# Six score banks of an attention kernel in three groups of two instead of four and two

## The chip, the cores and the metric

The kernel runs on one core of a Trainium2 chip. The metric is the time of one execution on the device in microseconds (us); less is better. The core's engines run side by side and meet through semaphores: TensorE (PE: matmuls, and PEld: the loading of their stationary operand), VectorE (DVE), ScalarE (ACT), GpSimd (POOL) and SyncE (SP), which issues most of the DMAs. An engine works through its own instructions in order.

## What is computed

The input is one sequence of 2048 tokens of width 128. After a layer norm two parts run on it, and both are added to the input: an attention of 16 heads of width 8, and a mixture of 8 experts with the best 2 for each token.

```python
q = proj(Wq) * mod
k = proj(Wk) * mod
v = proj(Wv) * mod
scores = jnp.einsum('bhid,bhjd->bhij', q, k) / math.sqrt(D)
scores = scores * cos_mat
w = jax.nn.softmax(scores, axis=-1)
w = (w + jnp.roll(w, 1, axis=-1)) / math.sqrt(2.0)
out = jnp.einsum('bhij,bhjd->bhid', w, v)
...
h1 = x_rep @ w1[e].T
a, g = jnp.split(h1, 2, axis=-1)
he = jax.nn.silu(a) * g @ w2[e].T
```

## The kernel before

**Scores.** A head's scores are 2048 x 2048, made in 64 tiles of 128 keys x 512 queries; 16 heads give 1024 tiles. One tile is one matmul (line 1381) with 49 rows of contraction, and fills one bank of PSUM. Two neighbours use different row halves of TensorE (`tile_position`) and run side by side, as a pair. Six banks, 0 to 5, hold scores; tile n goes to bank n % 6. Bank 6 is shared by all side work, bank 7 collects the weighted values.

**Exponentials.** ScalarE takes the exponential of a group of tiles with one ACTIVATE (line 706) out of PSUM and writes the result to one of 18 slots a tile in SBUF (`probs`). A round is six tiles, in two groups: a large one of four tiles (banks 0 to 3) and a small one of two (banks 4 and 5). There are 171 rounds; the last has four tiles.

**Weighted values.** TensorE multiplies the exponentials by the head's values (line 1402), four tiles (a quad) at a time in two halves, and adds them up in bank 7. In round r it takes pieces of tiles of rounds before r. At a head's end DVE copies the sums out (line 1046) and normalises them.

**Order.** Each engine's stream is written out round by round. TensorE in round r: `scores` of each group, a maximum job if one is due (line 1417: a score-like matmul of the last two heads, of which DVE takes the maximum, line 1065), then the pieces of weighted values, then the expert's step, then a second job in the rounds 27 to 44. From round 45 on, 39 tiles of tokens go through their experts, three rounds each: step 0 is the result of the tile before (line 1324) and, in 28 tiles, one job; step 1 is the first half of the wide matmuls (line 1311), after which ScalarE does a tanh (line 698); step 2 is the second half. ScalarE's stream: the exponentials of a round, then in step 1 the tanh.

**Waits.** TensorE's `scores(g)` waits until the exponentials up to group g - 2 are done (line 1372): the group that used the same banks in the round before. `weights(g)` on ScalarE waits for the scores of its group (`score_ready`, counted by groups) and until the probability slots are free (`pv_done`). TensorE's weighted values wait for `exp_done`, counted by `groups_for`. SP loads the operands of a head two heads ahead, in a round and behind a count of score groups that come from `groups_for` too (lines 518 to 521).

Of the kernel before, what the change touches and what calls it, by code (L numbers as in the profile page):

```python
# [55 lines left out]
ROWS = 2 * D  # L56
KQ = 1 + 3 * ROWS
HALF = S // 2
LARGE_GROUP, SMALL_GROUP = 4, 2
RING = LARGE_GROUP + SMALL_GROUP  # L60
PROBS = 3 * RING
PER_HEAD = NT * NC
SCORE_TILES = H * PER_HEAD
QUADS = PER_HEAD // NC
HALVES = 2
HW = CW // HALVES
SCORE_GROUPS = 2 * (SCORE_TILES // RING) + -(-(SCORE_TILES % RING) // LARGE_GROUP)
ROUNDS = -(-SCORE_TILES // RING)
SIDE_BANK = 6
V_BANKS = (7, 5)  # L70
# [52 lines left out]
def build(nc, x, Wq, Wk, Wv, Wo, phase, amp, wqkv, w1, w2, ident_in, desc_in, cs_in, sel_in, tri_in, below_in, count_in, heads_in, earlier_in, of_head_in, places_in, out):  # L123
# [3 lines left out]
    whole = nc.dram_tensor("whole_qk", [2, H, ROWS, S], F32, kind="Internal").ap()  # L127
# [7 lines left out]
    with ExitStack() as ctx:  # L135
# [3 lines left out]
        def sem(name):  # L139
            return ctx.enter_context(nc.semaphore(name))  # L140
# [143 lines left out]
        score_ready, exp_done, pv_done, vh_ready = (sem(n) for n in ("score_ready", "exp_done", "pv_done", "vh_ready"))  # L284
# [13 lines left out]
        def after(eng, signal, value):  # L298

            if not (isinstance(value, int) and value <= 0):  # L300
                eng.wait_ge(signal, value)

        def first_of(g):

            return min(RING * (g // 2) + LARGE_GROUP * (g % 2), SCORE_TILES)

        def group_tiles(g):

            return range(first_of(g), first_of(g + 1))

        def bank_of(n):

            return n % RING

# [13 lines left out]

        def groups_for(n):

            whole, rest = divmod(n, RING)
            return 2 * whole + -(-rest // LARGE_GROUP)

        def quads_for(n):

# [27 lines left out]
        def expert_step(r):  # L363

            m, step = divmod(r - EXPERTS_AT, ROUNDS_A_TILE)
            return (m, step) if 0 <= m <= TILES and step < 3 else (None, None)
# [5 lines left out]
        def rounds():  # L372

            done = 0
            for r in range(ROUNDS + 1):
                ready = min(RING * r, SCORE_TILES) // NC * HALVES
                head_ends = (done // (QUADS * HALVES) + 1) * QUADS * HALVES
                even = RING * HALVES * r // NC - 1
                pieces = range(done, max(min(ready if r == ROUNDS else min(ready, even), head_ends), done))
                done = pieces.stop  # L380
                yield r, jobs_of_round(r), pieces
            assert done == H * QUADS * HALVES
# [4 lines left out]

        def groups_of_round(r):

            return range(2 * r, min(2 * r + 2, SCORE_GROUPS))  # L390

        def load_operands(eng, h, q, k, half, loaded):

# [16 lines left out]
        def _(sp):  # L410
# [21 lines left out]
            def store_part(i, part):  # L432
                if part == 0:
                    sp.wait_ge(hi_ready, i + 1)
                else:
                    sp.wait_ge(parts_ready, i + 1)
                g, which = i // 2, i % 2
                sp.dma_start(scratch[which, 8 * g:8 * g + 8, part, :, :].rearrange("h r n -> r h n"),
                             parts[:, i, part, :]).then_inc(scratch_wr, 16)
# [4 lines left out]
            def load_head(p):  # L444
                sp.wait_ge(order_ready, 1 if p < EARLY else 2)
                sp.wait_ge(shift_wr, 16 if p < EARLY else 32)
                if p >= EARLY:
                    sp.wait_ge(scratch_wr, 8 * 16)
                h = sp.value_load(head_order[0:1, p:p + 1], min_val=0, max_val=H - 1)
                for half in range(2):  # L450
                    load_operands(sp, h, qa[p % 2], ka[:, p % 2, :], half, aug_ld[p % 2])
                    load_shift(p, h, half)
# [39 lines left out]
            def store_shifts(g):  # L492
                sp.wait_ge(shift_ready, g + 1)
                sp.dma_start(shift_rows[HALF_HEADS * g:HALF_HEADS * g + HALF_HEADS, :].rearrange("h (t p) -> (h t) p", p=P),
                             shift[:, g, :]).then_inc(shift_wr, 16)
# [19 lines left out]
            for r, _, _ in rounds():  # L515
                m, step = expert_step(r)
                for p in range(2, PLAIN):
                    issued = groups_for(PER_HEAD * (p - 1))
                    if r == -(-issued // 2):
                        sp.wait_ge(score_ready, issued)  # L520
                        load_head(p)
                if r - 1 in PARTS_AT:
                    for part in range(2):
                        store_part(2 + PARTS_AT.index(r - 1), part)
                if r == SECOND_AT + 4:
                    store_shifts(1)
                    sp.wait_ge(scratch_wr, 8 * 16)
                    sp.wait_ge(rows_ready, 2)
                    sp.wait_ge(order_ready, 2)
                    for i in range(EXACT):  # L530
                        h = sp.value_load(head_order[0:1, PLAIN + i:PLAIN + i + 1], min_val=0, max_val=H - 1)
                        for half in range(2):
                            load_operands(sp, h, qe[:, i, :], ka[:, 2 + i, :], half, exact_ld)
                if r == STAGE_AT:
                    for first in range(STAGES - 1):
                        stage_weights(first)
                if r == EXPERTS_AT - 2:
                    load_rows(0)
                    load_rows(1)
                    sp.dma_start(carried[:], slots_x[0:TILES * P, DM:WITH_PLACE].rearrange("(n p) k -> p n k", p=P)).then_inc(carried_ld, 16)  # L540
                if step == 1 and m + STAGES - 1 < TILES:
                    stage_weights(m + STAGES - 1)
                if step == 1 and m % 2 == 1 and m // 2 + 2 < ROW_PAIRS:
                    load_rows(m // 2 + 2)
                if r == EXACT_AT:
                    load_exact_shifts()
# [631 lines left out]
        def _(pe):  # L1178
# [190 lines left out]

            def scores(g):  # L1370

                after(pe, exp_done, g - 1)
                for n in group_tiles(g):
                    p, o, c, b = tile_at(n)
                    if n % PER_HEAD == 0 and p < PLAIN:
                        pe.wait_ge(aug_ld[p % 2], (p // 2 + 1) * 10 * 16)
                    elif n % PER_HEAD == 0:
                        pe.wait_ge(exact_shift_ld, EXACT * 2 * 16)
                    q, k = operands(p)
                    at = 64 * b  # L1380
                    ins = nc.tensor.matmul(ps[:, bank_of(n), :], k[at:at + KQ, P * o:P * o + P], q[at:at + KQ, CW * c:CW * c + CW],  # L1381
                                           start=True, stop=True, tile_position=(at, 0))
                ins.then_inc(score_ready, 1)
# [151 lines left out]
```

## Time and profile before

| | |
|---|---|
| Runs of the kernel | 579.5, 580.15, 581.8 us; median 580.15 |
| Profiled execution | 581.95 us, its span 580.1 us |
| TensorE, ScalarE, VectorE, GpSimd busy | 533.1, 506.9, 222.9, 92.8 us |
| Exponentials (line 706) | 341, busy 474.3 us |
| Granted TensorE clock, mean | 0.982 of full speed |

All durations come from the profiled execution. A busy share is an average; where ScalarE or TensorE sits idle before an instruction, a row's last column has that idle time and what ended it. Two instructions of one engine can overlap in the record, the end of one with the start of the next, so the distance between two starts is less than a duration.

### The profile page before, as it was taken

To read this page: it belongs to the slowest core of one execution; us is meant where nothing else is said; L and a number is where in the kernel's file an instruction comes from. 1 tells how busy PE (TensorE), PEld (TensorE's weight loads), DVE (VectorE), ACT (ScalarE), POOL (GpSimd) and SP (SyncE) were. 2 spreads that over 40 slices of the span, in tenths; PEclk is the share of its full clock that TensorE was granted. 3 is DMA by queue.
4 is the path that set the end of the run, shared out by engine and by line. 5 is a ranking of instruction groups with operands and counts; after the bars stand their busy time and mean duration, and the time that the engine had idled before them with its cause. 6 is when DMAs were issued, how large, how long until landed. Compare 5 with 4: busy or idle time off the path is not lost.

```text
span 580.1 us, 18927 instructions
## 1 busy us (share of the span) xinstructions
PE 533.1 (92%) x7964; PEld 260.2 (45%) x7964; DVE 222.9 (38%) x521; ACT 506.9 (87%) x411; POOL 92.8 (16%) x102
## 2 busy tenths in 40 slices
PE   2969999879999999999999999999999999999876
PEld 1442333323334555454554545555454555554325
DVE  6866356525445242323324232333323132132142
ACT  2649999979899899899999999999999999999971
POOL 5210266530000101011010101110110110101000
PEclk9978999989999999999999999999999999999997
DMA  7962054461014333233324333233324323300402
GB/s 219 193 181 79 20 139 115 110 195 47 2 40 67 88 106 96 88 97 96 97 71 113 98 95 97 86 97 88 106 80 104 98 54 97 92 13 11 139 13 76
DMA packets 60889, 53.75 MB, mean 93 GB/s; under 512 B 33244, under 2 KB 50294, under 8 KB 60546
## 3 DMA queue, kind: packets, MB, share of 16 engines
q1 hardware_dynamic: 58082, 47.48, 30.9%
q0 software_dynamic: 2272, 4.72, 2.3%
q8 instruction: 65, 1.06, 0.8%
q10 hardware_dynamic: 448, 0.30, 0.3%
q14 instruction: 22, 0.18, 0.1%
HBM read 38.68 MB, written 13.78 MB: 90 GB/s over the span
## 4 chain that ended last, share of the span: by engine, by line
PE 44%; issue 25%; ACT 21%; DVE 4%; DMA 2%; SPq 2%; ACTq 0%; DVEq 0%
PE ps L1402 20%; ACT big L706 20%; PE ps L1381 11%; PE ps L1324 4%; PE ps L1417 3%; PE ps L1200 1%; ACT cs L698 1%; PE ps L1351 1%; PE ps L1311 1%; DMA qk_parts<-store 1%; DVE store L789 1%; DMA acc<-in_L_attn_x 1%; DVE m L1065 1%; PE ps L1211 1%; PE ps L1188 1%
## 5 line engine op out<-in xcount | busy, mean ns | idle before, releaser
L706 ACT ACTIVATE big<-ps 128x2048 f32<-128x2048 f32 x341 | 474.3, 1463 | 35.5 <-PE ps L1381 27.8
L1402 PE MATMUL ps<-big,vh 128*32 128x256 f32 (+1 forms) x3968 | 258.5, 392 | 0.2 <-ACT big L706 0.2
L1402 PEld LDWEIGHTS ps<-big,vh 128*32 128x32 f32 x3968 | 111.8, 109 | 111.4 <-issue 57.6
L1381 PE MATMUL ps<-qa,ka 49*128 49x512 f16 x896 | 145.3, 387 | 17.5 <-ACT big L706 9.9
L1381 PEld LDWEIGHTS ps<-qa,ka 49*128 49x128 f16 x896 | 33.3, 94 | 112.6 <-ACT big L706 77.3
L604 POOL DMA_INDIRECT results<-y,row_of x39 | 37.8, 970 | 256.9 <-DVE y L1001 255.9
L986 DVE SCALAR_TENSOR_TENSOR cs<-cs,ps 128x384 f32<-128x384 f32 x39 | 21.6, 554 | 119.4 <-ACT cs L698 119.4
L1311 PE MATMUL ps<-xgT,store 128*32 128x128 f32 x1716 | 65.2, 273 | 0.2
L1065 DVE TENSOR_REDUCE m<-ps 128x1 f32<-128x512 f32 x64 | 44.2, 690 | 53.5 <-PE ps L1417 52.4
L1311 PEld LDWEIGHTS ps<-xgT,store 128*32 128x32 f32 x1716 | 54.0, 110 | 14.1 <-issue 1.1
L621 POOL DMA_INDIRECT slots_x<-attnT,slot x32 | 35.8, 1120 | 53.4 <-PE ps L1402 50.7
L995 DVE SCALAR_TENSOR_TENSOR cs<-cs,ps 128x384 f32<-128x384 f32 x39 | 21.6, 554 | 52.2 <-PE ps L1311 52.0
L1324 PE MATMUL ps<-store,cs 128*32 128x128 f32 (+1 forms) x936 | 32.8, 273 | 1.1 <-DVE m L1065 1.1
L1001 DVE TENSOR_SCALAR y<-ps,weight_of 128x128 f32<-128x128 f32 x39 | 13.4, 344 | 51.9 <-PE ps L1324 51.9
L1324 PEld LDWEIGHTS ps<-store,cs 128*32 128x32 f32 (+1 forms) x936 | 27.0, 110 | 8.4 <-issue 2.3
L1417 PE MATMUL ps<-ka,qe 49*128 49x512 f16 x64 | 24.6, 385 | 3.7 <-DMA ka<-qk_parts 2.3
L598 POOL COPY vh<-vaug 128x144 f32 x16 | 5.6, 352 | 129.6 <-PE ps L1402 112.2
L1381 PE MATMUL ps<-qe,ka 49*128 49x512 f16 x128 | 20.4, 382 | 3.4 <-ACT big L706 3.0
L698 ACT ACTIVATE cs<-ps 128x384 f32<-128x384 f32 x39 | 19.4, 497 | 1.1 <-PE ps L1311 1.1
L1046 DVE COPY osb<-ps 128x512 f32<-128x512 f32 x16 | 11.0, 690 | 19.7 <-PE ps L1402 19.5
L1417 PEld LDWEIGHTS ps<-ka,qe 49*128 49x128 f16 x64 | 5.9, 93 | 19.2 <-issue 8.8
L1055 DVE STREAM_TRANSPOSE osbT<-osb 128x512 f32<-128x512 f32 x16 | 11.4, 712 | 4.5 <-issue 3.5
(189 smaller groups left out, 217.6 us busy)
## 6 DMA issues: line engine op xcount, KB each, us to landing
store<-in_L_ffn_w SPq DMA_DIRECT2D x39, 352.0 KB, 3.2
store<-in_L_ffn_w SPq DMA_DIRECT2D x39, 192.0 KB, 3.3
qk_parts<-store SPq DMA_DIRECT2D x8, 512.0 KB
qa<-qk_parts SPq DMA_DIRECT2D x27, 128.0 KB
slots_x<-vh SPq DMA_DIRECT2D x8, 330.0 KB, 7.4
cs<-slots_x SPq DMA_DIRECT2D x80, 32.0 KB, 2.8
store<-results SPq DMA_DIRECT2D x4, 512.0 KB, 5.5
ka<-qk_parts SPq DMA_DIRECT2D x31, 64.0 KB
```

Source lines behind the costliest of these rows:

```text
L604: nc.gpsimd.indirect_dma_start(results, bass.IndirectOffsetOnAxis(ap=row_of[:, m:m + 1], axis=0), y[:, m % 4, :], None).then_inc(y_wr[m % ...
L621: nc.gpsimd.indirect_dma_start(slots_x, bass.IndirectOffsetOnAxis(ap=slot[:, r, t:t + 1], axis=0), xn_placed[:, t, :], None).then_inc(scat ...
L698: nc.scalar.activation(turned_gate[:, m % 2, :], ps[:, SIDE_BANK, 0:FP], ACT.Tanh, scale=0.5).then_inc(gate_ready, 1)
L706: nc.scalar.activation(probs[:, prob_of(tiles[0]):prob_of(tiles[-1]) + 1, :], ps[:, bank_of(tiles[0]):bank_of(tiles[-1]) + 1, :], ACT.Exp, ...
L986: nc.vector.scalar_tensor_tensor(turned_gate[:, k, :], turned_gate[:, k, :], 1.0, ps[:, SIDE_BANK, 0:FP], ALU.add, ALU.mult).then_inc(a_ta ...
L995: nc.vector.scalar_tensor_tensor(hidT[:, k, :, :].rearrange("p f s -> p (f s)"), turned_gate[:, k, :], 0.5, ps[:, SIDE_BANK, 0:FP], ALU.mu ...
L1065: nc.vector.tensor_reduce(m4[:, NT * h + i, c:c + 1], ps[:, SIDE_BANK, :], AX, ALU.max).then_inc(m_reduced, 1)
L1311: ins = nc.tensor.matmul(ps[c:c + 32, SIDE_BANK, P * f:P * f + P], w1_of[m % STAGES][:, F * b + f0 + c:F * b + f0 + c + 32], xgT[:, m % 2, ...
L1324: ins = nc.tensor.matmul(ps[c:c + 32, SIDE_BANK, FP:FP + DM], hidT[0:n, m % 2, f, c:c + 32], w2_of[m % STAGES][0:n, f, :], start=f == 0, s ...
L1381: ins = nc.tensor.matmul(ps[:, bank_of(n), :], k[at:at + KQ, P * o:P * o + P], q[at:at + KQ, CW * c:CW * c + CW], start=True, stop=True, t ...
L1402: ins = nc.tensor.matmul(ps[32 * c:32 * c + 32, O_BANK, cols], vh[:, p % 2, o + 8 * b, :], probs[:, prob_of(n), cols], start=k == 0, stop= ...
L1417: nc.tensor.matmul(ps[:, SIDE_BANK, :], qe[at:at + KQ, h, P * i:P * i + P], near_keys(ka[at:at + KQ, 2 + h, :], i), start=True, stop=True, ...
```

## The change

`first_of`, `groups_for` and `groups_of_round` count groups of two tiles, three a round. Each group has its own exponential, signal and wait: `scores(g)` now waits for group g - 3, which again is the group that used the same banks in the round before. Tiles, banks, slots, pieces of weighted values and every other step stay in the same order. The exponentials become 512 instead of 341.

```diff
-LARGE_GROUP, SMALL_GROUP = 4, 2
-RING = LARGE_GROUP + SMALL_GROUP
+GROUP_TILES = 2
+GROUPS_A_ROUND = 3
+RING = GROUP_TILES * GROUPS_A_ROUND
...
-SCORE_GROUPS = 2 * (SCORE_TILES // RING) + -(-(SCORE_TILES % RING) // LARGE_GROUP)
+SCORE_GROUPS = SCORE_TILES // GROUP_TILES
...
         def first_of(g):
-            return min(RING * (g // 2) + LARGE_GROUP * (g % 2), SCORE_TILES)
+            return GROUP_TILES * g
...
         def groups_for(n):
-            whole, rest = divmod(n, RING)
-            return 2 * whole + -(-rest // LARGE_GROUP)
+            return -(-n // GROUP_TILES)
...
         def groups_of_round(r):
-            return range(2 * r, min(2 * r + 2, SCORE_GROUPS))
+            return range(GROUPS_A_ROUND * r, min(GROUPS_A_ROUND * (r + 1), SCORE_GROUPS))
...
-                    if r == -(-issued // 2):
+                    if r == -(-issued // GROUPS_A_ROUND):
                         sp.wait_ge(score_ready, issued)
                         load_head(p)
...
             def scores(g):
-                after(pe, exp_done, g - 1)
+                after(pe, exp_done, g - GROUPS_A_ROUND + 1)
```

TensorE in step 0 of expert tile 10, before: the round's scores, the job, the weighted values and the result of the tile before.

```order
L1381 MATMUL ps<-qa1,ka 128x512 [waits exp_done]
L1381 MATMUL ps<-qa1,ka 128x512 x3
L1381 MATMUL ps<-qa1,ka 128x512 [waits exp_done]
L1381 MATMUL ps<-qa1,ka 128x512
L1417 MATMUL ps<-ka,qe 128x512 [waits hidT_ready,m_reduced]
L1402 MATMUL ps<-big,vh 32x256 x4
L1402 MATMUL ps<-big,vh 32x256 [waits exp_done]
L1402 MATMUL ps<-big,vh 32x256 x7
L1324 MATMUL ps<-store,cs 32x128 [waits m_reduced,y_copied,hidT_ready]
```

The same round after.

```order
L1381 MATMUL ps<-qa1,ka 128x512 [waits exp_done]
L1381 MATMUL ps<-qa1,ka 128x512
L1381 MATMUL ps<-qa1,ka 128x512 [waits exp_done]
L1381 MATMUL ps<-qa1,ka 128x512
L1381 MATMUL ps<-qa1,ka 128x512 [waits exp_done]
L1381 MATMUL ps<-qa1,ka 128x512
L1417 MATMUL ps<-ka,qe 128x512 [waits hidT_ready,m_reduced]
L1402 MATMUL ps<-big,vh 32x256 x4
L1402 MATMUL ps<-big,vh 32x256 [waits exp_done]
L1402 MATMUL ps<-big,vh 32x256 x7
L1324 MATMUL ps<-store,cs 32x128 [waits m_reduced,y_copied,hidT_ready]
```

The run of four score matmuls has been cut in two, with a wait of its own ahead of the second pair; all behind the scores stands as it stood.

ScalarE around one tanh, before.

```order
L706 ACTIVATE big<-ps 128x2048 [waits pv_done,score_ready]
L706 ACTIVATE big<-ps 128x1024 [waits pv_done,score_ready]
L698 ACTIVATE cs<-ps 128x384 [waits hidT_ready,a_ready]
L706 ACTIVATE big<-ps 128x2048 [waits pv_done,score_ready]
L706 ACTIVATE big<-ps 128x1024 [waits pv_done,score_ready]
```

And after, with the next tanh.

```order
L698 ACTIVATE cs<-ps 128x384 [waits hidT_ready,a_ready]
L706 ACTIVATE big<-ps 128x1024 [waits pv_done,score_ready] x9
L698 ACTIVATE cs<-ps 128x384 [waits hidT_ready,a_ready]
```

Between two tanhs stand nine exponentials of 1024 columns in place of three of 2048 and three of 1024.

## Rows read from the trace of the kernel before

**Rows 1.** The page: busy time of each engine; the line of the score matmuls.

```profile
PE 533.1 (92%) x7964; PEld 260.2 (45%) x7964; DVE 222.9 (38%) x521; ACT 506.9 (87%) x411; POOL 92.8 (16%) x102
...
L1381 PE MATMUL ps<-qa,ka 49*128 49x512 f16 x896 | 145.3, 387 | 17.5 <-ACT big L706 9.9
```

**Rows 2.** Expert and last stretch: us, busy PE, PEld, DVE, ACT, POOL, clock, DMA.

```profile
177.00:542.00 365.00, 356.34 (x6146) 185.83 (x6147) 109.58 (x253) 340.93 (x276) 40.47 (x49) 1.00 0.32 85
542.00:562.00 20.00, 17.82 (x237) 6.76 (x228) 5.96 (x12) 20.00 (x15) 0.56 (x1) 1.00 0.34 109
```

**Rows 3.** Waits of the expert stretch: waiter, waited for, us, times, longest.

```profile
PEld ps L1381 <- ACT big L706: 48.5, 94, 0.8
...
ACT big L706 <- PE ps L1381: 20.9, 38, 1.8
```

**Rows 4.** One expert tile in order of time: start, us, engine, line, idle before.

```profile
273.65 0.82 PE L1381 MATMUL ps<-qa,ka 49*128 49x512 f16 x6
...
274.29 2.79 ACT L706 ACTIVATE big<-ps 128x2048 f32<-128x2048 f32 x2 [0.49 <-PE ps L1381]
...
276.48 1.06 PE L1381 MATMUL ps<-qa,ka 49*128 49x512 f16 x6
...
277.14 0.10 PEld L1381 LDWEIGHTS ps<-qa,ka 49*128 49x128 f16 x2 [0.55 <-ACT big L706]
...
279.55 1.05 PE L1381 MATMUL ps<-qa,ka 49*128 49x512 f16 x6
...
280.21 0.10 PEld L1381 LDWEIGHTS ps<-qa,ka 49*128 49x128 f16 x2 [0.54 <-ACT big L706]
...
282.84 0.82 PE L1381 MATMUL ps<-qa,ka 49*128 49x512 f16 x6
```

**Rows 5.** ScalarE in the same tile, in narrow windows, one exponential a row.

```profile
276.07 1.02 ACT L706 ACTIVATE big<-ps 128x1024 f32<-128x1024 f32 x1
276.97 0.50 ACT L698 ACTIVATE cs<-ps 128x384 f32<-128x384 f32 x1
277.34 1.90 ACT L706 ACTIVATE big<-ps 128x2048 f32<-128x2048 f32 x1
...
279.10 1.06 ACT L706 ACTIVATE big<-ps 128x1024 f32<-128x1024 f32 x1
```

**Rows 6.** A tile without a maximum job: first and last score starts of it.

```profile
467.97 0.82 PE L1381 MATMUL ps<-qa,ka 49*128 49x512 f16 x6
...
476.95 0.82 PE L1381 MATMUL ps<-qa,ka 49*128 49x512 f16 x6
```

**Rows 7.** ScalarE never idle: three starts in narrow windows of the last rounds.

```profile
546.81 1.91 ACT L706 ACTIVATE big<-ps 128x2048 f32<-128x2048 f32 x1
...
548.57 1.07 ACT L706 ACTIVATE big<-ps 128x1024 f32<-128x1024 f32 x1
...
549.47 1.94 ACT L706 ACTIVATE big<-ps 128x2048 f32<-128x2048 f32 x1
```

**Rows 8.** Groups by shape: count, busy us, mean ns of one.

```profile
L706 ACT ACTIVATE big<-ps 128x2048 f32<-128x2048 f32 x171 | 322.9, 1888 | 35.5 <-PE ps L1381 27.8 <-issue 4.5
...
L706 ACT ACTIVATE big<-ps 128x1024 f32<-128x1024 f32 x170 | 175.9, 1035 | 0.0
```

**Rows 9.** ScalarE in the first 28 rounds, runs without idling and gaps (some).

```profile
47.75 13.54 ACT L706 ACTIVATE big<-ps 128x2048 f32<-128x2048 f32 x10 [0.19 <-PE ps L1381]
...
70.36 5.48 ACT L706 ACTIVATE big<-ps 128x2048 f32<-128x2048 f32 x4 [0.59 <-PE ps L1381]
```

**Rows 10.** Rounds with two jobs: start, us, engine, line, idle before.

```profile
161.61 0.39 PE L1417 MATMUL ps<-ka,qe 49*128 49x512 f16 x1
...
162.78 0.09 PEld L1417 LDWEIGHTS ps<-ka,qe 49*128 49x128 f16 x1 [0.30 <-DVE m L1065]
...
164.53 0.39 PE L1417 MATMUL ps<-ka,qe 49*128 49x512 f16 x1
```

**Rows 11.** ScalarE from 540 us to the last exponential.

```profile
541.48 18.91 ACT L706 ACTIVATE big<-ps 128x2048 f32<-128x2048 f32 x14 [1.29 <-PE ps L1381]
```

## The prediction

> **What bounds the kernel now.** I read the shares of busy time first. TensorE is busy for 92% of the span and ScalarE for 87% [rows 1]; neither number says which of the two ends last, so the table by stage comes next. I cut the score part into four stretches: the first 28 rounds (41 to 119 us), the rounds with two maximum jobs each (119 to 177), the 39 expert tiles (177 to 542) and the last rounds (542 to 562). Of the two that matter most [rows 2], the last has ScalarE busy for 20.00 of 20 us; in the expert stretch TensorE is busy for 356 of 365 us, ScalarE for 341, with the granted clock at 1.00 (2.4 GHz). The expert stretch is 63% of the span, so the change is decided there.
>
> Busy TensorE does not mean that TensorE alone sets the pace. In the waits of the expert stretch, TensorE's weight loads for scores wait 94 times for ScalarE, 48.5 us together, and ScalarE waits 38 times for TensorE's scores, 20.9 us [rows 3]. Each engine waits for the other, so what sets the pace is a loop through both. To see it I follow one expert tile (three rounds) in order of time [rows 4].
>
> - 273.65: TensorE starts six score matmuls of a round. The large exponential starts at 274.29, 0.64 later: four matmuls go as two pairs, then the hand-over. Six took 0.82 us and one takes 0.39 (the mean of its line [rows 1]), so a pair takes (0.82 - 0.39) / 2 = 0.215.
> - The small exponential starts at 276.07, 1.78 later. The tanh follows at 276.97 (0.90 later), the next large exponential at 277.34 (0.37 later) [rows 5]. Its small one starts at 279.10, 1.76 later.
> - TensorE's last score pair of the round after starts at 280.21, 1.11 after that small exponential began, because it waits until banks 4 and 5 have been read. It would have been ready at 279.55 + 0.43 = 279.98, so 0.23 is lost.
>
> The loop's first part is 0.64 + 1.78 + 0.90 + 0.37 + 1.76 + 1.11 = 6.56 = 280.21 - 273.65. From there TensorE works without a wait until 282.84, 2.63 us, when it begins the same round of the next tile. So a tile costs 9.19 us. After the maximum jobs end, the tile takes 476.95 - 467.97 = 8.98 [rows 6], by the same loop with 0.21 less work in its TensorE part. TensorE loses another 0.23 at 277.14 (ready at 276.48 + 0.43 = 276.91). Without both losses TensorE would need 8.73 a tile; ScalarE's own work is 3 x 2.66 + 0.37 = 8.35. The loop is longer than either.
>
> **The change in the expert stretch.** A round gets exponentials A, B, C of two tiles each. What the change moves is the first link: A needs one score pair instead of two, so it can start 0.64 - 0.215 = 0.43 after the pair. ScalarE waits at this place (0.49 idle before 274.29), so the earlier start counts. The last link stays: the third pair waits for C exactly as the small group's pair waited.
>
> What it adds is one exponential a round. Its price is the distance between starts, not the duration, since neighbours overlap. In the last rounds, where ScalarE is never idle, the large one starts at 546.81, the small at 548.57 and the next large at 549.47 [rows 7]: 1.76 and 0.90. The difference of 1024 columns is 0.86, so about 0.04 to 0.05 of each start is fixed. The tanh of 384 columns fits the same line: 384 x 0.833 ns + 50 ns = 370 ns, and 0.37 stands in the rows. (0.833 ns is (1888 - 1035) / 1024 from the mean durations [rows 8].) So three small ones take 3 x 0.90 = 2.71 with the unrounded 0.903, where a large and a small took 2.66: 0.05 more a round. A small one has never followed a small one in this trace; its bounds are 0.04 extra (the line above) and 1035 - 853 = 182 ns (no overlap at all). I take 0.05, since all three widths lie on that line.
>
> The loop after: 0.43 to A; 0.92 (after a wait a start costs 0.01 to 0.02 more, 1.78 against 1.76), 0.90, 0.90 to the tanh; 0.37; 0.90, 0.90 to the C of the next round; 1.11 to TensorE's pair. That is 6.43 against 6.56: 0.21 won, two extra exponentials at about 0.04 to 0.05 lost, **0.13 us a tile**. TensorE's part (2.63) is untouched, so a tile is 9.06, above TensorE's 8.73 and ScalarE's 8.50: no other limit takes over. Over 39 tiles: 39 x 0.13 = 5.1 us won. The cover: the tanh must find its matmuls done; these stand ahead of the scores that start at 276.48, and the tanh would be due at 276.97 - 0.21 + 0.05 = 276.8, a margin of about 0.3. If a head's end falls inside a tile, TensorE's part differs, but the same link opens the round.
>
> By the Trainium skill, page "ScalarE: Activation LUTs", section "What ACT_TABLE_LOAD costs", an ACTIVATE with immediates takes 186 ns and 0.833 ns a column, and neighbours overlap by about 93 ns. The slope is that of this trace; the net fixed part would be 93 ns a start, where the starts here leave 0.05. What that would make of the time is rival 1.
>
> **The first 28 rounds.** ScalarE runs long pieces without idling, such as ten exponentials in 13.54 us, with gaps between them, nine in all from 0.19 to 0.59, of which the first and the largest are shown [rows 9]. Where it never idles, the round grows by 0.05: at most 28 x 0.05 = 1.4 us. Each gap can shrink by 0.21 at most: 0.19 + 8 x 0.21 = 1.9, and the first start of all, which waits for a large group too, by some 0.3. Two or three gaps follow rounds in which TensorE did not wait for ScalarE, and there the earlier start is worth less. I take 0.6 won, with bounds of 2.2 won (no cost) and 1.4 lost (no gap helps).
>
> **The rounds with two jobs.** These last 2.92 us. The obvious loop is the one above without a tanh, and would shrink. But a second one has the same length: the job's matmul at 161.61, then DVE's reduction of it, the next job at 162.78, whose weight load the profile shows idle for 0.30 until DVE was done, and 1.75 later (164.53) the next first job [rows 10]: 1.17 + 1.75 = 2.92. The change touches neither part, so it keeps the period: **nothing won**, although A starts earlier. Bounds: 0.5 either way.
>
> **The last rounds.** Full ScalarE: eight rounds at 0.05 more, less 0.21 for the gap of 1.29 before 541.48 [rows 11]: 0.2 lost. The last round's four tiles become two small exponentials, one of those eight. The placement of the head loads stays: SP issues them in the same rounds, and waits for scores that come no later. The weighted values stand behind the same rounds' scores; DVE and GpSimd keep their order. The extra 171 waits and signals on TensorE cost nothing where they are already satisfied: at 273.65 all six score matmuls, the wait between them included, keep the 0.215 pitch.
>
> **Sum.** -5.1 - 0.6 + 0 + 0.2 = -5.5 us. The profiled execution took 581.95 us (span 580.1 and 1.85 around it), so it would take 576.4; the median of the three runs is 580.15, 1.8 below it, so the forecast is 580.15 - 5.5 = **574.6 us**.
>
> **Rivals.**
> 1. *Small behind small costs more, and eats the gain.* If only half of the 182 ns is hidden, an extra exponential costs 0.09: the tile wins 0.21 - 0.18 = 0.03 (-1.2), the first 28 rounds lose 2.5 - 2.2 = +0.3, the last +0.5. Together -0.4: **579.8 us**. For it: no small-small pair stands in the trace. Against it: small to large, small to tanh and tanh to large all fit 0.05. The Trainium skill's page "ScalarE: Activation LUTs" (section "What ACT_TABLE_LOAD costs"), with its 93 ns, would give this time.
> 2. *No overlap between small exponentials: slower.* Place: starts of B and C on ScalarE. Price 0.18: a tile +0.36 - 0.21 = +0.15, times 39 = +5.9; the first 28 rounds +5.0 - 2.2 = +2.8; the last +1.2: **590 us**. It decides the expert stretch from an extra of 0.105 an exponential. For it: the durations add up so (3 x 1035 against 1888 + 1035). Against it: every unstalled start overlaps its predecessor by 0.1 to 0.17.
> 3. *The stalls on TensorE vanish altogether.* If finer groups freed the banks in time, a tile would be 8.73: 39 x 0.46 = 18 us, **562 us**. Against it: the third pair still waits for C, and C starts after the same chain.
> 4. *The change doesn't do what it says*: A starts no earlier, because something other than the scores' signal holds ScalarE. Then 0.05 a round on ScalarE remains: 39 x 0.10 + 1.4 + 0.4 = +5.7, **586 us**. Against it: the profile names the scores for the idle time before the large one.
>
> **Chances.** Forecast 0.62 (its own range 572.8 to 577.2); rival 1 and cases near it 0.18; rival 2 0.05; rival 4 0.05; rival 3 and other larger gains 0.10. The range that should hold 8 in 10 reaches over rival 1: 571.5 to 581.0. A measurement of this kernel can tell 0.5% (2.9 us) from no change. Faster by more than that: 0.62 + 0.10 = 0.72. Within it: 0.18. Slower: 0.10.
>
> **What would show it.** In the changed kernel's profile: 512 exponentials, starts 0.90 apart where ScalarE is not idle (0.95 speaks for rival 1, over 1.0 for rival 2); A 0.43 after its pair in the expert stretch (0.64 speaks for rival 4); tiles of 9.06 and 8.86 us, the loss of 0.23 at the first of the two stalled rounds shrunk to about 0.05 while the other stays near 0.2 (rival 3: both gone); rounds with jobs still 2.92; unstalled ScalarE rounds 2.71. The forecast is wrong first if the fixed part of a start is off by 0.05, which moves a tile by 0.1 and the sum by 4 us and more.

## The result, and the profile after

The changed kernel takes **575.13 us** (median of four runs, 574.9 to 575.6), the kernel before on the same chip 580.14 (four runs, 579.5 to 581.8). By the medians it is 5.0 us faster (a quotient of 0.9914), where 5.5 were forecast. The ratios here and below are not quotients of the medians but come from all the runs compared; this one is 0.9901, with a 95% interval of 0.9874 to 0.9929. A second comparison with more runs stands under the experiments; one of its 24 runs of the kernel before took 665.2 us at a mean granted clock of 0.749, and is left out of the ratios there.

The changed kernel's page, and its windows over the expert tiles and the last rounds (stretch, its length, then busy us of TensorE, its weight loads, DVE, ScalarE and GpSimd, the granted clock, and what the DMA engines did):

```profile
span 573.8 us, 19271 instructions
...
PE 526.3 (92%) x7964; PEld 258.9 (45%) x7964; DVE 222.7 (39%) x521; ACT 513.2 (89%) x582; POOL 92.8 (16%) x102
...
L706 ACT ACTIVATE big<-ps 128x1024 f32<-128x1024 f32 x512 | 481.7, 1062 | 24.9 <-PE ps L1381 22.6
```

```profile
177.00:538.00 361.00, 352.84 (x6144) 185.65 (x6143) 109.42 (x253) 344.38 (x394) 40.34 (x49) 1.00 0.33 86
538.00:558.00 20.00, 17.53 (x237) 7.34 (x232) 6.21 (x12) 20.00 (x23) 0.81 (x1) 1.00 0.36 109
```

Against [rows 1, 2]: TensorE is busy for 6.8 us less in all, and ScalarE for 6.3 us more. The expert tiles and their neighbours shrank, and the picture within them is the old one: neither engine is full, which fits a loop through both that still sets the pace. In the waits of the expert stretch (waiter, waited for, us, times, longest) two lines tell it:

```profile
PEld ps L1381 <- ACT big L706: 48.9, 123, 0.8
...
ACT big L706 <- PE ps L1381: 14.0, 30, 1.7
```

ScalarE waits 6.9 us less for scores than in [rows 3], and TensorE waits as long for ScalarE as ever (48.9 against 48.5), now in 123 pieces instead of 94.

Now the same expert tile as in [rows 4], in order of time (start, length, engine and line, and in brackets the idle time before):

```profile
272.76 0.82 PE L1381 MATMUL ps<-qa,ka 49*128 49x512 f16 x6
...
273.19 2.86 ACT L706 ACTIVATE big<-ps 128x1024 f32<-128x1024 f32 x3 [0.36 <-PE ps L1381]
...
275.92 0.51 ACT L698 ACTIVATE cs<-ps 128x384 f32<-128x384 f32 x1
276.10 0.10 PEld L1381 LDWEIGHTS ps<-qa,ka 49*128 49x128 f16 x2 [0.40 <-ACT big L706]
276.29 5.64 ACT L706 ACTIVATE big<-ps 128x1024 f32<-128x1024 f32 x6
...
279.23 0.10 PEld L1381 LDWEIGHTS ps<-qa,ka 49*128 49x128 f16 x2 [0.61 <-ACT big L706]
281.86 0.82 PE L1381 MATMUL ps<-qa,ka 49*128 49x512 f16 x6
```

Narrow windows of ScalarE give single starts in between. The three exponentials of the round start at 273.19, 274.11 and 275.02; those of the next at 276.29, 277.19 and 278.10. The loop from 272.76 is 0.43 + 0.92 + 0.91 + 0.90 (tanh at 275.92) + 0.37 + 1.81 + 1.13 = 6.47, and TensorE's part is 281.86 - 279.23 = 2.63. So a tile is **9.10** (9.19 before, 9.06 forecast); without a job it is 8.89 (8.98 before, 8.86 forecast).

By stages the two profiled executions compare so. Each stage goes from the first score matmul of a round to that of another; the second row is a part of the first.

| stage | before | after | difference | forecast |
|---|---|---|---|---|
| rounds 0 to 27 | 85.11 | 84.57 | -0.5 | -0.6 |
| of it, last pair of round 3 to last pair of round 27 | 68.95 | 67.48 | -1.5 | |
| rounds 28 to 44, the jobs | 51.36 | 51.39 | 0.0 | 0 |
| rounds 45 to 162, the expert tiles | 364.29 | 360.42 | -3.9 | -5.1 |
| rounds 163 to 168 | 16.02 | 16.10 | +0.1 | +0.2 |
| from there to the end | 23.29 | 20.58 | -2.7 | 0 |

The spans differ by 6.4, the medians by 5.0. (The rows add up to 7.0; ahead of round 0, which no row holds, the profiled execution of after spent 0.6 more.) The last row is no effect of the change: the profiled execution of before had its TensorE clock at half for a while in that stage, and another execution of the same kernel took 20.35 there (below, the run before2). What the change did in these two profiles is -3.9 in the expert tiles and about -1.5 in the first rounds, and with the 0.1 lost near the end that makes -5.3, beside the 5.0 of the medians. The first figure comes back to 0.2 in every profile that bears on it; the second varies from execution to execution, as the run mixed shows.

### The profile page after: what moved, and what is told of

Its sections match the earlier page's. It is cut to its first block, busy times and chain, and to the rows that moved or that the text cites. A ratio compares the mean times of both kernels' runs of the same rounds, so it can differ in the third digit from the quotient of the medians.

```text
span 573.8 us, 19271 instructions
## 1 busy us (share of the span) xinstructions
PE 526.3 (92%) x7964; PEld 258.9 (45%) x7964; DVE 222.7 (39%) x521; ACT 513.2 (89%) x582; POOL 92.8 (16%) x102
## 4 chain that ended last, share of the span: by engine, by line
PE 59%; ACT 19%; issue 9%; DVE 8%; DMA 2%; SPq 2%; ACTq 0%; DVEq 0%
PE ps L1402 30%; ACT big L706 18%; PE ps L1381 12%; PE ps L1311 6%; PE ps L1324 4%; PE ps L1417 3%; DVE cs L995 2%; DVE m L1065 2%; PE ps L1200 2%; PE ps L1211 1%; DMA qk_parts<-store 1%; DVE store L789 1%; DMA acc<-in_L_attn_x 1%; PE ps L1351 1%; PE ps L1188 1%
## 5 line engine op out<-in xcount | busy, mean ns | idle before, releaser
L706 ACT ACTIVATE big<-ps 128x1024 f32<-128x1024 f32 x512 | 481.7, 1062 | 24.9 <-PE ps L1381 22.6
L1381 PE MATMUL ps<-qa,ka 49*128 49x512 f16 x896 | 142.2, 389 | 15.1 <-ACT big L706 9.2
L1381 PEld LDWEIGHTS ps<-qa,ka 49*128 49x128 f16 x896 | 34.7, 94 | 103.0 <-ACT big L706 72.0
```

What stands on the lines that cost most here:

```text
L706: nc.scalar.activation(probs[:, prob_of(tiles[0]):prob_of(tiles[-1]) + 1, :], ps[:, bank_of(tiles[0]):bank_of(tiles[-1]) + 1, :], ACT.Exp, ...
```

## Experiments

All kernels of one group were compared with the kernel before on the same chip; ratios are to it, with 95% intervals. The stage times are from one profiled execution each.

### Is the gain there again

The changed kernel, unaltered.

> The changed kernel once more. Theory (the loop): an expert tile takes 9.10 us with a maximum job and 8.89 without, against 9.19 and 8.98 before, since the first exponential starts 0.215 earlier and two extra ones cost 0.063 each, measured from end to end (not 0.045, as their starts suggest). The gain is then about 4 us in the expert stretch and 4.5 to 5 in all, a ratio of 0.991 to 0.993. The other 2.6 us by which the two profiles differ behind the last weighted values belong to the low clock that the profile of before shows there, and need not come back in another execution. Rival (the clock): the gain is partly a matter of the clock; then this run shows a low clock behind the last weighted values or a ratio beyond 0.995.

Measured: 575.43 against 580.52, ratio 0.9906 (0.9888 to 0.9924), just beyond the 0.991 to 0.993 that were expected. Expert tiles 360.43, tile 9.10, all within 0.01 of the first profile. The part from round 3 to round 27 is 67.51.

### What the early start is worth

The first exponential of each round waits until two pairs are there, as the large one did. The finer groups stay.

```diff
             def weights(g):
...
-                act.wait_ge(score_ready, g + 1)
+                act.wait_ge(score_ready, min(g + 2, SCORE_GROUPS) if g % GROUPS_A_ROUND == 0 else g + 1)
```

> Three groups of two, but ScalarE waits for two score pairs before the first exponential of a round, as the large group did. All else as in the changed kernel. Theory (the loop): the 0.215 us are gone and the price of the extra exponentials stays: a tile takes 9.10 + 0.215 = 9.32 us, 39 of them +8.4, and the short gaps of the first rounds return (up to 1): 583.5 to 584.5 us, slower than before by 0.7%. Rival (finer release): the gain comes from TensorE getting its banks back in smaller portions, not from the earlier start; then this stays at 575 to 576.

Measured: 584.62, ratio 1.0077 (1.0050 to 1.0105), slower than the kernel before. In its timeline:

```profile
275.18 0.82 PE L1381 MATMUL ps<-qa,ka 49*128 49x512 f16 x6
...
275.82 2.85 ACT L706 ACTIVATE big<-ps 128x1024 f32<-128x1024 f32 x3 [0.49 <-PE ps L1381]
...
281.86 0.10 PEld L1381 LDWEIGHTS ps<-qa,ka 49*128 49x128 f16 x2 [0.61 <-ACT big L706]
...
284.49 0.82 PE L1381 MATMUL ps<-qa,ka 49*128 49x512 f16 x6
```

The first exponential starts 0.64 after its pair, with the old idle time of 0.49. The rest of the loop is as after, and the tile is 284.49 - 275.18 = 9.31. Against 9.10 that is the full 0.215 of one score pair. So the gain of the change is the early start, and the extra exponentials are a pure cost: with the start undone, the expert tiles take 368.85, 4.6 more than before. The rival of that run, that the gain comes from the finer release of the banks, falls with it, since the release is as fine here. This gives the price of the cut without any reading of starts: (368.85 - 364.29) / 39 = 0.117 a tile, for two extra exponentials on the loop.

### Why three groups, and not the small one first

Two tiles, then four: the early start without an extra exponential. The groups come from a list (the same frame serves the next kernel and two later ones).

```diff
-GROUP_TILES = 2
-GROUPS_A_ROUND = 3
-RING = GROUP_TILES * GROUPS_A_ROUND
+RING = 6
+
+
+def sizes(r):
+    return 2, 4
...
             def scores(g):
...
-                after(pe, exp_done, g - GROUPS_A_ROUND + 1)
+                after(pe, exp_done, groups_for(first_of(g + 1) - RING))
```

> The two groups in the other order: two tiles, then four. No exponential more than before (341), and the first one needs one score pair only. Theory (the loop): what is won at the start (0.215) is lost at the end, because the last group of a round now has four tiles: TensorE's second and third pair wait for the end of a large exponential and then take 0.22 more. The loop is 0.43 + 0.92 + 1.77 + 0.37 + 0.90 + 1.97 + 0.22 = 6.58, the tile 9.21 us: 580 to 581.5 us, no gain over before. Rival (the early start alone is the gain): 39 x 0.215 = 8.4 less than before, 572 us.

Measured: 580.62, ratio 1.0003 (0.9983 to 1.0023): no change. Expert tiles 364.52.

```profile
274.90 0.82 PE L1394 MATMUL ps<-qa,ka 49*128 49x512 f16 x6
...
275.33 2.79 ACT L719 ACTIVATE big<-ps 128x1024 f32<-128x1024 f32 x2 [0.49 <-PE ps L1394]
...
281.24 0.11 PEld L1394 LDWEIGHTS ps<-qa,ka 49*128 49x128 f16 x4 [0.35 <-ACT big L719]
...
284.09 0.82 PE L1394 MATMUL ps<-qa,ka 49*128 49x512 f16 x6
```

The start is as early as after, 0.43, and the loop's first part is 281.24 - 274.90 = 6.34, 0.22 less than before. But behind the last release there are now two pairs (x4) where there was one (x2): TensorE's part is 284.09 - 281.24 = 2.85 where it was 2.63, and the tile is 9.19 again. The early start is paid back at the release, to the hundredth. The gain of the change needs both ends small: the first group, so that ScalarE starts early, and the last, so that little is left to do once it is read.

### A last group of one tile

The other half of that thought, `return 2, 2, 1, 1`: only one score tile waits for the last exponential, for one more exponential a round.

> Four groups a round, of 2, 2, 1 and 1 tiles: one exponential a round more than in the changed kernel, 683 in all, with first link and last release where they were. Theory (the loop, price by ends): each extra exponential costs 0.063, a tile 2 x 0.063 = 0.127 more, 39 of them 5.0, and the rounds in which ScalarE never idles another 2.2: 582.3 us. By the distance of starts (0.050) it would be 580.6. Rival (exponentials are cheap, the clock made the difference): 575 to 577.

Measured: 580.15, ratio 0.9995 (0.9972 to 1.0019), from ten runs between 577.7 and 583.6. The total lies 2.1 below the 582.3 expected by ends and beside the 580.6 expected by starts, so it does not decide between the two prices; the stages do. The tile without a job is 9.01 against 8.89, the round in which ScalarE never idles 2.81 against 2.75. Both fit 0.06 for each extra exponential. With a job the tiles alternate between 9.23 and 9.09, where after has 9.10. By its program the job of every other tile takes the row half that the last single score leaves free. In such a tile its job starts 0.11 behind that score's weight load (274.85 and 274.74), in the next 0.23 (284.07 and 283.84), and the cost of the extra exponentials is gone in every other tile; that is why the total came out lower. The release won nothing, as a reading: one score tile took as long as two that run side by side. The expert tiles take 363.57, 3.2 more than after and 0.7 less than before, and in the total nothing is left that can be told from no change.

### Are the rounds with two jobs held by the jobs

The forecast of no gain there said that the chain job, reduction, job sets 2.92. Here the second job goes ahead of the last piece of weighted values.

```diff
-                for u in pieces:
+                last = pieces[-1:] if jobs[1] else pieces[:0]
+                for u in pieces[:len(pieces) - len(last)]:
                     weighted_values(u)
                 expert_work(r)
                 for j in jobs[1]:
                     max_job(j, None)
+                for u in last:
+                    weighted_values(u)
```

> The changed kernel, but in the rounds with two maximum jobs the second job goes ahead of the last piece of weighted values, not behind it. Nothing is left out or added. Theory (the job loop holds these rounds at 2.92 us in both kernels: job, DVE's maximum of it, next job 1.17 later, and 1.75 to the one after): with 0.4 to 0.5 us of matmuls moved into the first distance DVE is done in time, and the rounds fall to what ScalarE needs or the exponential loop gives, 2.75 to 2.80. 15 of them: 1.8 to 2.5 us less than the changed kernel, 573 us. Rival (the rounds are held by the exponentials): they stay at 2.92 and the time at 575.4.

Measured: 580.35 against 581.57, ratio 0.9974 (0.9945 to 1.0004), a miss of some 7 us. The rounds are no longer 2.92; they alternate between 2.86 and 2.91. So the chain of jobs did hold them, but only by 0.01 to 0.06, and the next limit stands right behind it: the job now sits between two pieces of weighted values. Before, the second job starts 0.06 after DVE's reduction ends (162.72 and 162.78); here it starts 0.21 after (161.67 and 161.88), so the reduction no longer holds it. The total says little of the edit. Five of the ten runs took 577.3 to 578.6 at a mean granted clock of 0.983 to 0.985, the other five 582.1 to 584.4 at 0.971 to 0.979, and the profiled execution is one of the latter. Its stage took 53.90 instead of 51.39, but 1.7 of these 2.5 lie in round 28, where its clock was at half until 131.8, 4.9 us into the stage (in after 1.9 us); 24.22 in the last stage is the matter of the next run. Even the faster five miss the 573 by over 4 us. The period of the rounds is what the run shows: that the jobs hold them is supported, not more.

### The tail of the kernel before

The kernel before once more, for one profile.

> The kernel before once more, for a second trace of it. Theory: its score part is as in the first trace (from the first score matmul of the round after the jobs to that of the round after the expert tiles 364.3 us, tiles of 9.19 and 8.98). The time from the last round's scores to the end was 23.3 us in the first trace, with the clock at 1.2 GHz for 6.8 us in the middle of the output projection, and 20.4 to 20.6 in the five traces since, where that stretch began later. If that is chance, this trace can show 20.5 too; if it belongs to the kernel before, it shows 23 again and 2.6 us of the gain are the clock's.

Measured: the stage after the last rounds takes 20.35 us, where the first profile of the same kernel has 23.29. Windows of both, first two from the first profile and then one from this one; the third number from the end (0.55, 0.60; 1.00) is the granted clock:

```profile
566.00:570.00 4.00, 3.44 (x21) 3.01 (x19) 0.99 (x4) 2.34 (x4) 0.00 (x0) 0.55 0.00 0
570.00:574.00 4.00, 4.00 (x24) 4.00 (x24) 1.37 (x2) 0.00 (x0) 0.00 (x0) 0.60 0.21 62
```

```profile
568.00:572.00 4.00, 3.12 (x27) 2.85 (x28) 1.45 (x6) 2.05 (x4) 0.00 (x0) 1.00 0.00 0
```

The first profile spent 6.8 us at 1.2 GHz in the output projection, just behind a stretch in which TensorE had little to do (1.4 of 4 us busy from 562 on); this one did the same work at 2.4 GHz. Over all twelve profiles of this study, of whatever kernel, the stage takes 20.3 to 20.8 us in eight, 21.7 in one (best), and 23.3 to 24.2 in three (before, job_early, fill222). The expert tiles of both profiles of before agree to 0.01 (364.29 and 364.30). So the 2.7 us in the last row of the table above belong to the execution.

### Fill the stall with other work

TensorE loses time at the last pair of two rounds of a tile, because it waits for an exponential. Here the first piece of weighted values goes between the last two groups of scores, once with four and two tiles (fill42) and once with three groups (fill222).

```diff
             for r, jobs, pieces in rounds():
-                for g in groups_of_round(r):
+                groups = list(groups_of_round(r))
+                early = pieces[:1] if groups else pieces[:0]
+                for g in groups[:-1]:
+                    scores(g)
+                for u in early:
+                    weighted_values(u)
+                for g in groups[-1:]:
                     scores(g)
...
-                for u in pieces:
+                for u in pieces[len(early):]:
                     weighted_values(u)
```

> The kernel before, groups of four and two, with one move on TensorE: the round's first piece of weighted values (some 0.45 us, which needs nothing of this round) goes between the large and the small group's scores, in all rounds. Theory (the loop): TensorE no longer waits for the small exponential, the work stands where the wait was, and an expert tile falls to what TensorE needs: 8.73 us with a job, 8.51 without, 0.46 less. 39 tiles give 18 us, the rounds with two jobs fall from 2.92 to about 2.7 (3.5 us): 558 to 564 us. Rival (the wait comes back behind the moved work, or ScalarE sets the pace at 9 us a tile): 572 us or more.

> The same move in the changed kernel: the round's first piece of weighted values between the second and the third group's scores. Theory: the loop through ScalarE no longer sets the pace, so three groups have nothing left to win: the expert tiles are TensorE's 8.73 and 8.51 to 8.6 as with groups of four and two, and the extra exponentials cost 0.06 a round where ScalarE never idles, now also in the rounds with two jobs: 1.5 to 4 us slower than the kernel with four and two and the same move, 561 to 567 us. Rival (three groups are better by themselves): faster than it by 3 to 5 us.

Measured: 594.63 and 594.95 against 581.57, ratios 1.0229 (1.0205 to 1.0253) and 1.0217 (1.0192 to 1.0242). The stall is gone and the kernels are 13 us slower than before, some 30 slower than expected. Two rounds of fill42:

```profile
266.95 0.16 PEld L1402 LDWEIGHTS ps<-big,vh 128*32 128x32 f32 x8 [0.42 <-ACT big L706]
...
267.52 0.10 PEld L1381 LDWEIGHTS ps<-qa,ka 49*128 49x128 f16 x2 [0.41 <-issue]
...
269.81 0.61 PE L1381 MATMUL ps<-qa,ka 49*128 49x512 f16 x4
270.34 0.16 PEld L1402 LDWEIGHTS ps<-big,vh 128*32 128x32 f32 x8 [0.42 <-issue]
270.34 0.64 PE L1402 MATMUL ps<-big,vh 128*32 128x256 f32 x8
...
270.91 0.10 PEld L1381 LDWEIGHTS ps<-qa,ka 49*128 49x128 f16 x2 [0.41 <-issue]
270.92 0.39 PE L1381 MATMUL ps<-qa,ka 49*128 49x512 f16 x2
271.23 0.59 PEld L1402 LDWEIGHTS ps<-big,vh 128*32 128x32 f32 x16 [0.23 <-issue]
...
272.89 0.61 PE L1381 MATMUL ps<-qa,ka 49*128 49x512 f16 x4
```

The word "issue" says that nothing the profile shows was waited for. The six score matmuls used to stand together, 0.82; now they come as 0.61 and 0.39, and the change from one kind to the other and back happens twice a round. This round takes 272.89 - 269.81 = 3.08 where 2.83 stood before (276.48 - 273.65 in [rows 4]): **0.25 us** for one more change to weighted values and back. Three rounds of it would cost 0.75, and the two stalls of 0.23 gave 0.46, so 0.29 is to be expected; the tile grew by 0.26 without a job. With a job it grew by 0.36: the round that holds the job takes 269.81 - 266.42 = 3.39, 0.33 more than the 3.29 of before less its stall of 0.23. Both groupings come to the same tile, 9.55, and 9.24 without a job, and their totals are 0.3 apart, within their intervals, where 1.5 to 4 were expected. That is the second reading of this pair: where TensorE alone sets the pace, cutting the groups finer gains nothing, since the start of ScalarE is then on no path.

### Each round with the grouping that suits it

Three groups only in the expert tiles; four and two in the others (mixed).

```diff
...
+def sizes(r):
+    return (2, 2, 2) if EXPERTS_AT <= r < EXPERTS_AT + 3 * TILES else (4, 2)
...
```

> Three groups of two in the expert tiles only; four and two in the other 54 rounds. Theory (the loop): the expert tiles stay at 9.10 and 8.89; between the last score pair of the 4th round and that of the 28th the time returns from 67.5 us to the 69 to 70 of the kernel before, since the short waits of ScalarE there shrank with the earlier start too; the last rounds win back 0.06 each. In all 1 to 2 us more than the changed kernel: 576.5 us. Rival (outside the tiles the extra exponentials only cost): 574.5 us or less.

Measured: 576.94 against 580.86, ratio 0.9934 (0.9912 to 0.9956). The expert tiles take 360.42, exactly as after; the part from round 3 to round 27 takes 68.82, as before (68.95), and not 67.5. So the gain in the expert tiles stands by itself.

How large the one in the first rounds is, is less sure. Seven profiles run these rounds in one of the two groupings with nothing else changed there: with three groups they take 67.49 (after), 67.51 (again), 68.51 (best) and 68.80 (job_early), with four and two 68.95 (before), 69.79 (before2) and 68.82 (mixed). The means are 68.1 and 69.2, a gain of 1.1, but within each grouping the executions spread by 1.0 to 1.3, and two with three groups come close to mixed. Nor do the totals tell mixed from the changed kernel: the intervals of their ratios overlap.

The last kernel puts four and two into the third round of each tile, whose first exponential ScalarE starts without idling, and into the last rounds, where it never idles (best). Everywhere else three groups stay.

```diff
...
+def sizes(r):
+    in_tiles = EXPERTS_AT <= r < EXPERTS_AT + 3 * TILES
+    return (4, 2) if r >= EXPERTS_AT + 3 * TILES or in_tiles and (r - EXPERTS_AT) % 3 == 2 else (2, 2, 2)
...
```

> Three groups of two, except where the first exponential of a round starts behind the tanh without waiting for scores (the last round of each expert tile) and in the last rounds, where ScalarE never idles: four and two there. Theory (the loop, price by ends): one extra exponential less in the loop gives 0.06 us a tile, tiles of 9.04 and 8.83, 39 of them 2.4 us, and the last eight rounds 0.4: 572.6 us, faster than the changed kernel by 0.5%. Rival (the large group there comes late, since it needs a second score pair which waits for a bank): no gain or a loss, 575 us or more.

Measured: 574.12 against 580.86, ratio 0.9894 (0.9866 to 0.9921). The tile is 9.03 and 8.82, the expert stretch 358.51, 1.9 less than after (2.4 were expected for one extra exponential a tile less on the loop). Its timeline has the same steps as after, with a last link that closes 0.07 earlier:

```profile
272.06 0.82 PE L1395 MATMUL ps<-qa,ka 49*128 49x512 f16 x6
...
278.46 0.10 PEld L1395 LDWEIGHTS ps<-qa,ka 49*128 49x128 f16 x2 [0.55 <-ACT big L720]
...
281.09 0.82 PE L1395 MATMUL ps<-qa,ka 49*128 49x512 f16 x6
```

The loop is 278.46 - 272.06 = 6.40, against 6.47. Its median is the lowest of all, but the intervals of its ratio and of the changed kernel's overlap, so only the stage time shows the gain, not the whole.

## Why the prediction came out right, and which terms did not

**The loop.** The reading that both engines wait for each other, and that only the link from the first score pair to the first exponential moves, held link by link. The start came 0.43 after its pair, TensorE's part stayed at 2.63, no other limit took over. late_a and g24 show it from both sides: without the early start the kernel is slower than before, and without the small last group the early start is worth nothing. Rivals 3 and 4 fall, 3 because both losses on TensorE are still there, 4 because the start did come earlier.

**The price of an exponential: mis-sized.** This was the term named as the first to go wrong. 0.13 a tile was forecast and 0.09 measured in the tiles that follow the loop. The stage gave 3.9 and not 5.1; that is 0.10 a tile, since some of the others won 0.15 to 0.4 (8.94 to 8.68 in one) and a few lost 0.1 to 0.2. The step that failed is "its price is the distance between starts". In the last rounds of the changed kernel, where ScalarE never idles, the whole run and the first and the seventeenth of its exponentials read:

```profile
537.51 21.19 ACT L706 ACTIVATE big<-ps 128x1024 f32<-128x1024 f32 x23 [1.00 <-PE ps L1381]
```

```profile
537.51 1.03 ACT L706 ACTIVATE big<-ps 128x1024 f32<-128x1024 f32 x1 [1.00 <-PE ps L1381]
...
552.00 1.21 ACT L706 ACTIVATE big<-ps 128x1024 f32<-128x1024 f32 x1
```

Sixteen starts lie 14.49 apart, 0.906 each. The ends, 538.54 and 553.21, lie 14.67 apart: 0.917 each. The duration grows from 1.03 to 1.21 while nothing about the work changes. TensorE is released by ends, and it sees them: in the expert tile above, the third exponentials end at 276.05 and 279.18, and TensorE's waiting loads start at 276.10 and 279.23, 0.05 later. In the last rounds a round is 2.75, three times 0.917, where it was 2.69. So three small ones cost 0.06 more than a large and a small, not 0.045; that late_a gives 0.117 a tile for two is the same number by another road. The mean duration on the page of the profile (1062 ns, against 1035 in [rows 8]) fits this growth. In the loop it shows as 1.81 for two starts instead of 1.80, 0.91 for one, and 1.13 for the last link instead of 1.11.

Rival 1 had 0.09 for the price and 579.8 for the time; both are outside what was measured. The Trainium skill, page "ScalarE: Activation LUTs", section "What ACT_TABLE_LOAD costs", has 186 ns for an ACTIVATE with immediates and an overlap of 93, from which one would estimate 186 - 93 = 93 ns of each exponential beside its columns. The ends here leave 917 - 853 = 64 ns and the starts 51 to 53: this case's trace has less than that estimate by either measure, and the forecast's 50 ns was nearer to both.

**The two losses on TensorE.** One did shrink, from 0.23 to about 0.08, as forecast. The other was to stay near 0.2 and grew to 0.29 (the pair's load at 279.23, ready at 278.51 + 0.43 = 278.94). Most of that was already in the forecast's own loop: TensorE is ready 0.17 earlier (the first loss shrinks by that) and the last link comes 0.13 earlier, so the second loss had to grow by 0.04, to 0.27; only then is a tile 9.06, 0.33 above TensorE's 8.73. The rest is the creep again: the third exponential of the second round ends later than its start says.

**The first 28 rounds: mis-sized, the other way.** The forecast summed the idle times before large exponentials and let each shrink by 0.21 at most. From round 3 on the gain was 1.5 in the first pair of profiles and 1.1 in the mean of seven, not 0.6 for all 28. Idle time in the record is less than what ScalarE lost there. One round of before, and one of after, each a row for the last work of the round and one for the first of the next:

```profile
96.54 2.85 ACT L706 ACTIVATE big<-ps 128x2048 f32<-128x2048 f32 x2
...
99.70 1.88 ACT L706 ACTIVATE big<-ps 128x2048 f32<-128x2048 f32 x1 [0.31 <-PE ps L1381]
```

```profile
101.71 1.14 ACT L706 ACTIVATE big<-ps 128x1024 f32<-128x1024 f32 x1
...
102.83 1.02 ACT L706 ACTIVATE big<-ps 128x1024 f32<-128x1024 f32 x1
```

Before, that round lasted 99.70 - 96.54 = 3.16, 0.50 more than the unstalled 2.66, while the row shows 0.31 of idle time: where two exponentials would overlap, the record calls the overlap no idle time. After, the starts are 1.12 apart instead of 0.90 and the row shows no idle time at all. (Part of such a distance is the creep of the ends, which is paid there.) From the first exponential of round 3 to that of round 27 it is 68.95 before and 67.40 after, which exceeds 24 unstalled rounds by 68.95 - 24 x 2.66 = 5.1 and by 67.40 - 24 x 2.71 = 2.4. So 2.7 of stall went, for 24 x 0.05 = 1.2 of extra exponentials. The forecast had bounded the gain by the idle times in the rows, eight of them from there on with 3.1 together, where 5.1 were lost. That the whole of rounds 0 to 27 shows only 0.5 has at least in part another cause: the profiled execution of after was still at half clock (0.50) between 48 and 52 us, where that of before had the full one (1.00), and its ScalarE idled for 1.21 right ahead of round 3. From the last score pair of round 2 to that of round 3 it took 4.09, where again, at the full clock from 47.8 us on, took 2.75. The window of after:

```profile
48.00:52.00 4.00, 4.00 (x30) 1.31 (x32) 3.73 (x9) 2.79 (x4) 0.00 (x0) 0.50 0.01 4
```

The second profile of after has 84.16, that of before 86.32. Single executions do not settle this sum, and the part from round 3 on settles it only to about 1 us, as the seven profiles under mixed show.

**The jobs and the last rounds.** Nothing won in the one (51.36 and 51.39, rounds of 2.92), 0.1 lost in the other where 0.2 was forecast. Both as they were worked out.

So the total was right partly by luck, because two mis-sized terms cancelled: 1.2 too much in the expert tiles, 0.5 to 0.9 too little in the first rounds.

## What to carry to other kernels

When two engines wait for each other, write the loop down link by link and ask which link a change shortens and which it lengthens. Splitting a group pays at the end where the consumer is idle (here the first group) only if the end where the producer is released stays small too, and it costs one fixed part of an instruction for each cut. Size that fixed part by the distance between ends over a long run without idling, and size a stall by the excess of a start distance over the unstalled one, not by the idle time in the row.

## What the runs showed of the hardware that was not expected

- Back-to-back exponentials of 128 x 1024 start 0.904 to 0.906 us apart and end 0.917 apart; their recorded duration grows from 1.03 to 1.21 us over 16 of them, and begins again at 1.02 after a stall, even one too short to be shown. Whether the growth is in the engine or only in the record was not tried; the released engine follows the ends, 0.05 behind.
- One more change on TensorE from score matmuls (49 rows, f16) to weighted values (128 rows, 32 columns, f32) and back costs 0.25 us a round. It shows as 0.20 to 0.42 of "issue" ahead of the weight loads; what in the engine takes it was not tried.
- At the end of the kernel TensorE's clock is at 1.2 GHz for 6.8 us of the output projection in one execution, and at 2.4 GHz throughout it in another of the same kernel; the stage takes 23.29 and 20.35 us. A single profile's span is uncertain by that much here.
